# The last node stage and the batch norm as one unrolled stage, with column sums by TensorE and the output stored by block in three parts

## The reference

```
def _L3(h, ef, gamma, beta, src, dst):
    z = h[src] + h[dst] + ef
    mean, mean_sq = segment_sum(z) / deg, segment_sum(z * z) / deg
    std = sqrt(relu(mean_sq - mean * mean) + 1e-5)
    mx, mn = segment_max(z), segment_min(z)
    agg = concatenate([mean, mx, mn, std])
    amp, att = agg * (log(deg + 1) / AVG_D), agg * (AVG_D / log(deg + 1))
    hc = concatenate([h, agg, amp, att]).reshape(N, 13, d).mean(axis=1)
    mu, var = hc.mean(axis=0), hc.var(axis=0)
    return (hc - mu) / sqrt(var + 1e-5) * gamma + beta
...
h = jnp.maximum(_layernorm(x, axis=-1), 0.0)
x = x + _L3(h, edge_attr_64, L3_gnn_gamma, L3_gnn_beta, src, dst)
return x
```

## Time and profile before

| | us |
|---|---|
| median of 3 runs | 14495.62 |
| lowest and highest of them | 14492.58, 14495.76 |
| the profiled execution: its time | 14492.5 |
| its span (first to last recorded work) | 14490.8 |
| GpSimd busy in it | 10110.2 (70%) |
| VectorE busy | 7035.3 (49%) |
| ScalarE busy | 3988.9 (28%) |
| TensorE busy | 791.2 (5%) |
| DMA, mean over the span | 91 GB/s |

### The profile page before, as it was taken

One profiled execution on the slowest core, in us unless ns is written; L12 is line 12 of the kernel. 1 busy time (PEld: TensorE's weight loads), 2 busy tenths in 40 slices (PEclk: granted clock), 3 DMA queues, 4 the chain that ended last, 5 costly groups with the idle time before them and its releaser, 6 DMA issues. The chain is left out here.

```text
span 14490.8 us, 55109 instructions
## 1 busy us (share of the span) xinstructions
PE 791.2 (5%) x3365; PEld 680.8 (5%) x3365; DVE 7035.3 (49%) x10457; ACT 3988.9 (28%) x3610; POOL 10110.2 (70%) x10617
## 2 busy tenths in 40 slices
PE   1000002200000720000010000010000000000000
PEld 1000002200000610000010000000000000000000
DVE  5677776477777223333323333332333336555554
ACT  0233332233333112222212222211111114655550
POOL 4777776677777267777767777767777766777762
PEclk9999999555555555555555555555555555555555
DMA  7444443344444012222212222212222223444441
GB/s 301 110 119 119 119 119 84 95 118 118 119 119 116 17 50 62 62 62 62 61 35 59 59 59 57 59 39 56 59 59 57 59 51 108 150 154 151 152 149 51
DMA packets 1013584, 1323.19 MB, mean 91 GB/s; under 512 B 703068, under 2 KB 720988, under 8 KB 993452
## 3 DMA queue, kind: packets, MB, share of 16 engines
q0 software_dynamic: 342560, 386.08, 14.0%
q1 hardware_dynamic: 586028, 400.31, 10.0%
q10 hardware_dynamic: 84960, 536.42, 9.3%
HBM read 660.45 MB, written 661.55 MB: 91 GB/s over the span
## 5 line engine op out<-in xcount | busy, mean ns | idle before, releaser
L1397 POOL DMA_INDIRECT c_y<-g_tab,c_at x4704 | 4465.7, 949 | 1530.0 <-issue 1499.1
L718 POOL DMA_INDIRECT c_y<-h_tab,c_at x3136 | 2959.4, 944 | 1002.4 <-issue 974.3
L1767 POOL DMA_INDIRECT c_y<-h_tab,c_at x1568 | 1479.5, 944 | 580.6 <-issue 544.7
L1432 DVE TENSOR_TENSOR c_s<-c_y,c_ad 128x64 f32<-128x64 f32 x294 | 78.6, 267 | 3629.8 <-DMA c_y<-g_tab,c_at 3629.8
L1472 DVE TENSOR_TENSOR_SCAN c_acc<-c_r,c_w_in 128x1156 f32<-128x1156 f32 x294 | 754.2, 2565 | 10.2
L751 DVE TENSOR_TENSOR c_prod<-c_y,c_q_all 128x1552 f32<-128x1552 f32 x196 | 347.1, 1771 | 837.9 <-DMA c_y<-h_tab,c_at 837.9
L741 DVE TENSOR_TENSOR_SCAN c_q_all<-c_mask,c_q_in 128x408 f32<-128x408 f32 (+1 forms) x784 | 732.9, 1003 | 28.8 <-issue 21.6
L782 DVE TENSOR_TENSOR_SCAN c_acc<-c_r,c_w_in 128x408 f32<-128x408 f32 (+1 forms) x784 | 732.0, 996 | 6.7
L1492 ACT ACTIVATE c_ex<-c_de 128x64 f32<-128x64 f32 x294 | 66.9, 228 | 2411.4 <-DVE c_de L1459 2410.3
L1502 ACT ACTIVATE c_row<-c_acc 128x1088 f32<-128x1088 f32 x294 | 618.9, 2105 | 0.0
L805 ACT ACTIVATE c_q_in<-c_q_raw 128x1552 f32<-128x1552 f32 x196 | 599.1, 3057 | 59.7 <-DVE c_q_in L732 59.7
(11 more groups left out here) (327 smaller groups left out, 6595.2 us busy)
## 6 DMA issues: line engine op xcount, KB each, us to landing
rows_d<-c_row ACTq DMA_DIRECT2D x98, 2048.0 KB, 6.9
rows_d<-c_row ACTq DMA_DIRECT2D x294, 576.0 KB, 2.9
rows_d<-c_row ACTq DMA_DIRECT2D x196, 784.0 KB, 3.3
c_q_raw<-q_start SPq DMA_DIRECT2D x196, 776.0 KB, 4.4
q_start<-setup_zero SPq DMA_DIRECT2D x49, 1552.0 KB, 9.1
c_y<-h_tab,c_at POOLq DMA_INDIRECT x4704
c_y<-g_tab,c_at POOLq DMA_INDIRECT x4704, 2.5
c_y<-in_edge_attr SPq DMA_DIRECT2D x196, 256.0 KB
```

The lines of the kernel that those rows point to most:

```text
L718: nc.gpsimd.indirect_dma_start(y[:, b, k, 0:D], None, h_tab, indexed(at[:, b, k:k + 1]))\
L1397: nc.gpsimd.indirect_dma_start(y[:, b, k, :], None, g_tab, indexed(at[:, b, k:k + 1]))\
L1767: nc.gpsimd.indirect_dma_start(y[:, b, k, :], None, h_tab, indexed(at[:, b, k:k + 1]))\
```

## The change

The two stages become one (`finish_pna`), `batch_norm` goes, and the loop over blocks is written out.

- SyncE loads all indices at once. The gathers go into three buffers, `got` [P, 3, 14, 256]; from the fourth block on GpSimd waits until the step `min` of the block three back is done, not for its end.
- `mean` and `msq` are PSUM tiles of two banks each; 1/degree (`rdeg`) and `beta` lie in a PSUM tile `small`. The square of the mean is ScalarE's. One step is added, `xb`: x + beta, by block.
- TensorE multiplies each block of h by ones as soon as its step `h13` is done, at most 8 columns (512 elements) a matmul, adding up in PSUM `sum_ps` over all blocks. Places that hold no node are left out by taking 127 rows from column 54 on; the cuts with `valid` go. VectorE sums the eight columns that are left.
- Subtracting the mean, squaring and the second sum go block by block over VectorE, ScalarE and TensorE. So does scaling: h times scale for a block, x + h for the block ahead.
- After each block's x + h SyncE stores it in three parts: partitions 0 to 111, partitions 112 to 126, and for the first four blocks the nodes of partition 127.

The one store of 127 rows has become seven of 112 rows and seven of 15, each pair behind its own block. The diff, in which `...` marks what is left out:

```diff
@@ -1932,61 +1933,122 @@
     def finish_pna(tag, rows):
+        NBUF, W = 3, NW * D
+        blocks = [slice(g * NW, (g + 1) * NW) for g in range(NWBLK)]
+        full = N_NODES // NC
+        rest = N_NODES - full * NC
         st = Stage(nc, tag, signals)
...
+        at = st.sb("at", [P, NC], I32)
+        got = st.sb("got", [P, NBUF, NW, 4 * D])
+        ld, fac = (st.sb(n, [P, NC]) for n in ("ld", "fac"))
+        t, sq = st.sb("t", [P, NW, D]), st.sb("sq", [P, NC, D])
+        gb, mu, sc = st.sb("gb", [P, 2, D]), st.sb("mu", [P, D]), st.sb("sc", [P, D])
+        mean, msq = (st.ps(n, [P, 1024])[:, 0:W].rearrange("p (k f) -> p k f", k=NW) for n in ("mean", "msq"))
+        small, sum_ps, sq_ps = (st.ps(n, [P, 512]) for n in ("small", "sum_ps", "sq_ps"))
+        rdeg, beta = small[:, 0:NC], small[:, NC:NC + D]
+        loaded, at_loaded = st.dma("w_loaded", 32), st.dma("at_loaded0", 16)
+        stored = st.dma("out_stored", 16 * (2 * NWBLK + rest // NW + 1))
+        node_got = [st.dma(f"block_got{b}", 16 * NW * len(blocks[b::NBUF])) for b in range(NBUF)]
+        pre = st.chain("pre_steps", "deg1 rdeg beta ln none none2 inv amp fac1 fac2 fac3")
+        names = "mean msq sq var relu root max min h3 std fac h13 xb".split()
         steps = st.sem("node_steps", len(names) * NWBLK)
...
+        summed, centred, squared, sq_summed, scaled, written = (st.sem(n, NWBLK) for n in (
+            "col_summed", "col_centred", "col_squared", "col_sq_summed", "col_scaled", "col_written"))
+        ch = st.chain("bn_steps", "sum mu sum2 var root inv scale")
         def before(g, name):
             return steps(g * len(names) + names.index(name))
+        def after(g, name):
+            return steps(g * len(names) + names.index(name) + 1)
+        def pieces(cols):
+            lo = cols.start
+            while lo < cols.stop:
+                hi = min(cols.stop, lo + 8, rest if lo < rest else NC)
+                yield slice(lo, hi), P if hi <= rest else full
+                lo = hi
         with nc.Block() as block:
             @block.sync
             def _(sp):
...
+                sp.dma_start(at[:], last_d).then_inc(at_loaded.h, 16)
+                sp.dma_start(gb[:, 0, :], row_of(a["L3_gnn_gamma"], D)).then_inc(loaded.h, 16)
+                sp.dma_start(gb[:, 1, :], row_of(a["L3_gnn_beta"], D)).then_inc(loaded.h, 16)
+                by_part = out[0:full * NC, :].rearrange("(p c) f -> p c f", p=full)
+                tail = out[full * NC:N_NODES, :].rearrange("(p c) f -> p c f", p=1)
+                cut = full // 16 * 16
+                for g, cols in enumerate(blocks):
+                    sp.wait_ge(*written(g + 1))
+                    sp.dma_start(by_part[0:cut, cols, :], x[0:cut, cols, :]).then_inc(stored.h, 16)
+                    sp.dma_start(by_part[cut:full, cols, :], x[cut:full, cols, :]).then_inc(stored.h, 16)
+                    if cols.start < rest:
+                        own = slice(cols.start, min(cols.stop, rest))
+                        sp.dma_start(tail[:, own, :], x[full:full + 1, own, :]).then_inc(stored.h, 16)
+                sp.wait_ge(*stored(16 * (2 * NWBLK + rest // NW + 1)))
             @block.gpsimd
             def _(pool):
...
+                pool.wait_ge(*at_loaded(16))
+                pool.nop(nofuse=True)
+                for g, cols in enumerate(blocks):
+                    if g >= NBUF:
+                        pool.wait_ge(*after(g - NBUF, "min"))
+                        pool.nop(nofuse=True)
                     for k in range(NW):
...
+                        c = cols.start + k
+                        nc.gpsimd.indirect_dma_start(got[:, g % NBUF, k, :], None, rows, indexed(at[:, c:c + 1]))\
+                            .then_inc(node_got[g % NBUF].h, 16)
...
                 act.activation(ld[:], deg[:], ACT.Ln, bias=ones[:, 0:1], scale=1.0).then_inc(pre.h, 1)
-                def body(i, b):
-                    act.wait_ge(*before(i * 2 + b, "root"))
+                for g in range(NWBLK):
+                    act.wait_ge(*before(g, "sq"))
+                    act.activation(t[:], mean, ACT.Square).then_inc(steps.h, 1)
+                    act.wait_ge(*before(g, "root"))
                     act.activation(t[:], t[:], ACT.Sqrt, bias=eps[:]).then_inc(steps.h, 1)
-                over_wide_blocks(act, body)
+                for g, cols in enumerate(blocks):
+                    act.wait_ge(*centred(g + 1))
+                    act.activation(sq[:, cols, :], h[:, cols, :], ACT.Square).then_inc(squared.h, 1)
+                act.wait_ge(*ch.before("root"))
+                act.activation(sc[:], sc[:], ACT.Sqrt, bias=eps[:]).then_inc(ch.h, 1)
+            @block.tensor
+            def _(pe):
+                def add_columns(total, values, cols):
+                    for part, rows_ in pieces(cols):
+                        n = (part.stop - part.start) * D
+                        last = nc.tensor.matmul(total[:, 0:n], ones[0:rows_, :],
+                                                values[0:rows_, part, :].rearrange("p c f -> p (c f)"),
+                                                start=part.start == 0, stop=part.stop == NC)
+                    return last
+                for g, cols in enumerate(blocks):
+                    pe.wait_ge(*after(g, "h13"))
+                    pe.nop(nofuse=True)
+                    add_columns(sum_ps, h, cols).then_inc(summed.h, 1)
+                for g, cols in enumerate(blocks):
+                    pe.wait_ge(*squared(g + 1))
+                    pe.nop(nofuse=True)
+                    add_columns(sq_ps, sq, cols).then_inc(sq_summed.h, 1)
...
                 v.wait_ge(*pre.before("deg1"))
-                v.tensor_scalar(rdeg[:], deg[:], 1.0, None, ALU.max).then_inc(pre.h, 1)
+                v.tensor_scalar(rdeg, deg[:], 1.0, None, ALU.max).then_inc(pre.h, 1)
                 v.wait_ge(*pre.before("rdeg"))
-                v.reciprocal(rdeg[:], rdeg[:]).then_inc(pre.h, 1)
+                v.reciprocal(rdeg, rdeg).then_inc(pre.h, 1)
+                v.wait_ge(*loaded(32))
+                v.wait_ge(*pre.before("beta"))
+                v.tensor_copy(beta, gb[:, 1, :]).then_inc(pre.h, 1)
                 v.wait_ge(*pre.before("none"))
                 v.tensor_scalar(fac[:], has[:], -1.0, 1.0, ALU.mult, ALU.add).then_inc(pre.h, 1)
@@ -2004,117 +2066,72 @@
                 v.scalar_tensor_tensor(out=fac[:], in0=fac[:], scalar=1.0 / 13.0, in1=has[:],
                                        op0=ALU.mult, op1=ALU.mult).then_inc(pre.h, 1)
                 v.wait_ge(*pre.upto(len(pre)))
...
+                for g, cols in enumerate(blocks):
+                    b = g % NBUF
                     rd = rdeg[:, cols].unsqueeze(2).to_broadcast([P, NW, D])
                     s_, q_, mx, nmn = (got[:, b, :, D * k:D * (k + 1)] for k in range(4))
-                    v.wait_ge(*node_got[b](i * (16 * NW) + 16 * NW))
+                    v.wait_ge(*node_got[b](16 * NW * (g // NBUF + 1)))
                     v.wait_ge(*before(g, "mean"))
-                    v.tensor_tensor(mean[:], s_, rd, ALU.mult).then_inc(steps.h, 1)
+                    v.tensor_tensor(mean, s_, rd, ALU.mult).then_inc(steps.h, 1)
                     v.wait_ge(*before(g, "msq"))
...
+                    v.tensor_tensor(msq, q_, rd, ALU.mult).then_inc(steps.h, 1)
                     v.wait_ge(*before(g, "var"))
-                    v.tensor_tensor(t[:], msq[:], t[:], ALU.subtract).then_inc(steps.h, 1)
+                    v.tensor_tensor(t[:], msq, t[:], ALU.subtract).then_inc(steps.h, 1)
                     v.wait_ge(*before(g, "relu"))
                     v.tensor_scalar(t[:], t[:], 0.0, None, ALU.max).then_inc(steps.h, 1)
                     v.wait_ge(*before(g, "max"))
-                    v.tensor_tensor(msq[:], mean[:], mx, ALU.add).then_inc(steps.h, 1)
+                    v.tensor_tensor(msq, mean, mx, ALU.add).then_inc(steps.h, 1)
                     v.wait_ge(*before(g, "min"))
-                    v.tensor_tensor(msq[:], msq[:], nmn, ALU.subtract).then_inc(steps.h, 1)
+                    v.tensor_tensor(msq, msq, nmn, ALU.subtract).then_inc(steps.h, 1)
                     v.wait_ge(*before(g, "h3"))
-                    v.scalar_tensor_tensor(out=msq[:], in0=h[:, cols, :], scalar=3.0, in1=msq[:],
+                    v.scalar_tensor_tensor(out=msq, in0=h[:, cols, :], scalar=3.0, in1=msq,
                                            op0=ALU.mult, op1=ALU.add).then_inc(steps.h, 1)
                     v.wait_ge(*before(g, "std"))
-                    v.tensor_tensor(msq[:], msq[:], t[:], ALU.add).then_inc(steps.h, 1)
+                    v.tensor_tensor(msq, msq, t[:], ALU.add).then_inc(steps.h, 1)
                     v.wait_ge(*before(g, "fac"))
-                    v.tensor_tensor(msq[:], msq[:],
-                                    fac[:, cols].unsqueeze(2).to_broadcast([P, NW, D]), ALU.mult)\
```

(73 more changed lines are left out.)

70 lines of the change are left out of this document (2 added, 68 removed).

## The result

| | before | after |
|---|---|---|
| median | 14494.1 us (14492.2 to 14495.8, 4 runs) | 14329.7 us (14328.3 to 14330.6, 4 runs) |
| profiled execution: time, span | 14492.5, 14490.8 | 14329.0, 14327.1 |

The ratio is 0.9887, 95% interval 0.9869 to 0.9904: 164 us less, where 157 were forecast. The time lies in the range, 9 us under the predicted 14339 and 1.7 above the range's lower end of 14328.

A forecast was written before the change was run, and what follows sets the result against it. The end was taken as bound by a one-engine store, GpSimd's gathers and one-engine-at-a-time passes; gains 117.2 + 10 + 0.1 + 29.3 = 156.6 us give span 14334.2, forecast 14339 us with run offset. Forecast range 14328 to 14357; 80% range 14326 to 14366.

The forecast's parts named there:

- gathers: Node stage, GpSimd's 98 gathers: 123.4 us, a gain of 10, since VectorE's additions and products keep at most one SBUF operand.
- last block to its h: Node stage, VectorE's exposed last block: 12.9 us to its h for 12.95 before, with x + beta beside TensorE.
- TensorE, last block of the first pass: Column sums: the first pass hides under the gathers except for the last block, 3.0 + 0.25 us.
- second pass: TensorE's sum of squares: 16.75 us, four blocks at 3.0, three at 1.5 and 0.25; bounds 10.5 and 21.
- small steps: Behind the second pass: 1.0 us for the sum and 1.56 for scale, root, inverse and gamma, 2.56 together.
- scaling: Last stage on VectorE: fourteen operations of 896 elements at 1.12 us each, 15.7 us, for 20.1 in three passes.
- store: End of the kernel: 127 rows use one DMA engine; stored by block, 3.0 us for 120.2, a gain of 117.2.
- PSUM operands: VectorE's node-stage operations: no cost taken for PSUM operands; by the skill's figures an estimate of 0.065 us each.
- VectorE as the bound: Rival, 10%: PSUM operands make VectorE bound the node stage, 20.0 us a block, about 14358; at twice the price 14392.
- the store on one engine in spite of the cut: Rival, 5%: it is not the 127 rows that confine the store, so 118 us run from the first block's end; 14443.
- TensorE at its upper bound: Rival, 5%: TensorE takes 42 us for 16.5 in the second pass and 3 more in the first; 14368.
- SyncE held: Rival "Slower", 2%: each block's stores hold the next on SyncE's queue 53.84 us, six holds 323 us for 13.5; 14648.

The follow-up runs named there:

- both PSUM experiments: Changed kernel with mean, msq, 1/degree and beta in SBUF: gathers 139.3 us; kernel before with mean, msq and 1/degree in PSUM, square on ScalarE: 124.0.
- the run with more matmuls: Changed kernel with two more 128x512 matmuls ahead of TensorE's second pass: that pass 10.8 us for 12.5, last h to last addition's end 33.8 for 35.5.
- The run with the stores further apart: Changed kernel with the last-but-one block's addition put ahead of the last block's scaling: end 3.9 us behind the last addition, 0.5 us less in all.
- The changed kernel without the cut: Changed kernel with each block's store as one DMA of 127 rows: 124.8 us from first issue to span's end for 15.5; total 14453 us.
- the two runs of the store alone: Kernel before with its one store cut at partition 112, or at 125: 13.5 and 26.9 us from issue to end, spans ending at 14399.7 and 14399.0.

## Why the prediction was right, step by step

The steps of the forecast, with what the trace of after has for each:

| step | forecast us | measured | where |
|---|---|---|---|
| start of the gathers | as before, 14151.6 | 14149.4 | not of the change |
| gathers | 123.4 | 123.0 | confirmed by both PSUM experiments |
| last block to its h | 12.9 | 12.8 | 14274.26 to 14287.09 |
| TensorE, last block of the first pass | 3.25 | 3.5 | 14287.09 to 14290.58 |
| sum and mean | 1.26 | 0.96 | |
| centre and square | 2.1 | 2.2 | |
| second pass | 16.75 | 12.5 | 14293.76 to 14306.26 |
| small steps | 2.56 | 2.2 | to 14308.44 |
| scaling | 15.7 | 14.15 | to 14322.59 |
| store | 3.0 | 4.5 | to 14327.1 |

- **Store, right in mechanism, 1.5 us short.** That one engine in sixteen carried it was the largest term, 117 of 157 us. The tail was read as one issue and one landing. Left out were the second issue of the block (0.43), what lies between landing and the span's end (about 0.4, in the tail of before too), and the block before it: the last two additions stand next to one another, so two blocks of 0.46 MB are issued within 2 us. By the Trainium skill ("DMA: Bandwidth & Descriptors", on why a DMA increments its semaphore by 16), 125 rows would go to five engines. By that rule, the trace agrees: 133 GB/s and a share of 0.31, where 127 rows had 26 and 0.06.
- **Gathers, right, and shown.** The argument from a single pair of rows carried. The Trainium skill ("SBUF — State Buffer", section "SBUF: two separate sides") states that VectorE and GpSimd share a port pair by an exclusive lock, and that a VectorE operation with two SBUF inputs takes it against a GpSimd operation that reads SBUF; the pair 14262.34 and 14262.42 agrees, in that the gather reads its indices from there. Only one side of such a lock is seen: in the same trace gathers that begin 0.04 to 0.17 us ahead of such an operation take 0.95, and VectorE's operation behind them isn't held either, 1.09 as ever.
- **PSUM operands, taken at no cost, cost under 0.01 us a step.** The seven steps a block that write to PSUM take 1.095 to 1.099 us, the three that only read from it 1.086 to 1.092 (1.092 with SBUF alone). The estimate of 0.065 us from the Trainium skill ("VectorE: DVE Perf Modes", the errata table) doesn't hold here. VectorE was never near a bound: it waited 3.7 us for the gathers at the last block.
- **Second pass, too long by 4.25.** The step that failed is "I take the middle, four blocks at 3.0 and three at 1.5". At the full clock the pass takes 10.8 us (the run with more matmuls); the 1.7 over that are half the time spent at half the clock, 3.4 us and not 12, and the stretches show the same: 0.50 from 14293.8 to about 14297. The stage of the earlier trace rows, where it stayed at 0.50 for 16 us with TensorE busy, was no guide; what sets it apart from this pass was not found.
- **Scaling, too long by 1.55.** 1.12 us a step came from rows where each step waits for the one ahead. Here an operation needs the one before the last; they start 1.00 us apart and overlap. The run with the stores further apart has both in a row: 1.00 from 14320.14 to 14321.14, where the second needs nothing of the first, and 1.12 from 14321.14 to 14322.26, where the addition needs the scaling just ahead.
- **The total.** -4.25, -1.55 and -0.3 in the small terms, +1.5 at the store, and -0.5 in gathers and last block make 5.1 us less than forecast; another 2.2 came from an earlier start of the stage, which the change didn't make. Their sum, 7.3, stands for the 7.1 by which the span is shorter than 14334.2 (the rest is rounding). Without the early start, which was luck, the time would be about 14332.
- **The rivals.** VectorE as the bound, the store on one engine in spite of the cut, TensorE at its upper bound and SyncE held didn't come. The changed kernel without the cut shows SyncE's holds alive, seven issues of 5.7 to 17.3 us; but the end is set by the one engine's 118 us of transfer, not by a sum of holds as that rival had it.

## What to carry to other kernels

Read the DMA share of a long transfer against one sixteenth first: here 127 rows cost 118 us where all the passes ahead of them took 71, and one cut gave 107 back. Where indirect gathers from GpSimd are the bound, put one operand of each VectorE operation that runs beside them in PSUM: 9 to 10 of 133 us here. When a pass is split to overlap with a store, count every issue of a block and what the block before still has in the queue, and price the steps by whether each waits for its neighbour.

## What the runs showed that was not expected

**The same gathers, 0.15% slower in some executions.** The page's groups by line for the changed kernel and for the one with two gather buffers, same code up to the last stage:

```profile
L1398 POOL DMA_INDIRECT c_y<-g_tab,c_at x4704 | 4465.3, 949 | 1529.9 <-issue 1500.8
L719 POOL DMA_INDIRECT c_y<-h_tab,c_at x3136 | 2959.1, 944 | 1002.9 <-issue 974.8
```

```profile
L1398 POOL DMA_INDIRECT c_y<-g_tab,c_at x4704 | 4472.8, 951 | 1529.6 <-issue 1500.4
L719 POOL DMA_INDIRECT c_y<-h_tab,c_at x3136 | 2963.9, 945 | 1002.1 <-issue 979.0
```

7.5, 4.8 and 2.2 us (the third group, of 1,568) make 14.5 of the 16.7 us by which the last stage began later there. The mean gather is 1 to 2 ns longer; why, no run tells, and of the two runs of the store alone on the same chip, one began its last stage at 14166.9 and the other at 14152.9. It is as large as a tenth of what the change brought, and enough to turn a single comparison of totals: of these two the one with the store 13 us longer had the shorter total.

**A second operation that needs nothing of the first** starts 1.00 us behind it on VectorE although each is recorded with 1.08 to 1.10 us for 896 elements.

**The clock's rise differs between executions of one kernel**: the second pass of the changed kernel took 12.5 us in one and 13.4 in another.
